# A decoder layer for two sequences: the loop over sequences written out as one straight program

## The chip, the cores and the metric

The kernel runs on one core of a Trainium2 chip. The metric is the device time of one execution in microseconds (us), median of three runs. A core has TensorE (PE, matrix products into eight accumulator banks of 128 x 512 fp32), VectorE (DVE), ScalarE (ACT), GpSimd (POOL) and SyncE (SP, which here only issues DMAs). Each engine has its own instruction stream, and they wait for each other through semaphores.

## What is computed

A post-layernorm decoder layer on x of 2 x 1024 x 256, all in fp32: causal self-attention with rotary embedding (16 heads of 16), cross-attention to 77 context tokens, and a gated feed-forward network of hidden width 1024 with ternary weights (times 8) and a scale for each output row. Each part is added to its input and normalised.

```python
x = _layernorm(x + attn(x, w_qkv, w_proj))          # softmax((q k^T)/4 under a causal mask) v
x = _layernorm(x + xattn(x, ctx, mask, Wq, bq, ..., Wo, bo))
# feed-forward, _tlin(x, w, s) = (x @ w.T) * s
h = silu(_tlin(x, w1_w, w1_s)) * _tlin(x, w2_w, w2_s)
h = gelu(_tlin(h, h1_w, h1_s))
h = gelu(_tlin(h, h2_w, h2_s))
x = _layernorm(x + _tlin(h, w3_w, w3_s))
```

## The kernel before, in words

`decoder_layer` sets up buffers and semaphores and runs a loop, `nc.Fori(0, BATCH)`, whose body `build_sequence` holds the whole work of one sequence for all five engines. Each turn begins after an all-engine barrier that also clears the semaphores. The body has these stages, on every engine in the same order:

- Projections. For each of 8 token tiles PE makes q and k (`project_qk`, L456, 512 wide) and, five tiles later, v (`project_v`, L463); the context's k and v (L470) come in between and are turned (`turn_ctx`). DVE applies the rotary embedding (`rope`, L980 to L982) and adds the context's biases and stages its k (`ctx_add`, L987 to L999); ACT copies v (`v_evac`, L849) and the turned context (`ctx_evac`, L857).
- Self-attention, in numbered steps. The heads go in 8 pairs. For a pair PE turns q and k (L507) and computes the raw scores once for the row maxima (L521, 24 units of up to 512 columns for each pair: "max units"). DVE reduces each unit (`reduce_unit`: L1028 where the whole bank is taken, L1030 with the causal mask and then a read of its accumulator). The first two pairs are done ahead of the first scores: the warm-up. `unit_bank` deals these 48 units over `SHARED` = 6 banks, and all later ones over banks 0 and 1, since banks 2 to 5 then hold scores. After the warm-up PE computes the scores again, transposed (L550), ACT takes their exp (L878), POOL clears above the diagonal (L1280), and PE multiplies by v (L567). Output projection, residual and layernorm of each token tile (`norm_products`, `norm_work`, `norm_evacs`) are put on fixed steps near the end of the attention.
- Cross-attention, built in the same way, with 3 max units for each pair, and its own projections and layernorms; the last four token tiles of those are interleaved with the first feed-forward products.
- Feed-forward in two chunks of 512 tokens. All operands are split into a high and a low part in a narrower type (fp32r), and each product is two matmuls of 512 columns (L733 for w1 and w2, L749 for h1 and h2, L761 for w3). A chunk has 36 groups, one bank each, taken in turn from six: 16 for w1 and w2 alternately (4 matmuls each), 8 for h1 and 8 for h2 (16 each), and 4 for w3 (16 each). ACT applies silu (L954) or gelu (L964), DVE multiplies silu by the second product (`gate`, L1224) and rounds to the high part (L1164), POOL subtracts for the low part (L1326). For w3, DVE multiplies by the scale (L1243), adds the residual (L1245), takes statistics (L1078, L1080), POOL makes the reciprocal root (`rstd`, L1286 to L1289), and DVE finishes (L1085), one tile later in its own order.

In the first turn alone, DVE looks through all feed-forward weights for bits that fp32r would lose (`check_piece`, L1074, 22 pieces) and every engine skips this by an `If(b == 0)` in the second turn. The weights (5.5 MB) are then resident in `ffn_w`. If bits were found, the feed-forward products run in fp32 on the same operands. The next sequence's tokens and context are loaded by SP while the last feed-forward products run.

## Time and profile before

| what | value |
|---|---|
| median of the runs | 972.98 us (972.43 to 979.55, 3 runs) |
| profiled execution | 979.19 us, of which its span (first to last instruction) 977.8 |
| TensorE busy | 882.5 us (90%), mean granted clock 0.895 |
| VectorE busy | 538.2 us (55%) |
| ScalarE busy | 364.8 us (37%) |
| GpSimd busy | 363.0 us (37%) |
| data moved | 34.61 MB |

The span can be cut into 40 equal slices. In the page's second section each digit is the busy share of a slice in tenths, and PEclk is the clock that TensorE was granted, in tenths of full speed:

```profile
PE   5879999888889999999968789999998889999997
DVE  3596788767676711441145967886167774116113
PEclk9965999769986999999979668997999699999999
DMA  9909201000000000000020000010000000000000
```

The first sequence takes slices 1 to 20 or so and the second the rest. The granted clock is given as a fraction of 2.4 GHz, so 0.5 is the lower of its two levels, 1.2 GHz, and a stretch with 0.74 is a mix.

### The profile page before, as it was taken

What the parts mean: (1) busy time and instruction counts of PE and PEld (TensorE: products, weight loads), DVE (VectorE), ACT (ScalarE), POOL (GpSimd) and SP (SyncE); (2) the same over time, 40 slices, a digit from 0 to 9 for tenths busy, and PEclk for the clock granted to TensorE, in tenths of its full rate; (3) what the DMA queues carried; (4) which work ended last, traced back from release to release, by engine and by line L of the source; (5) the groups of instructions that cost most, each with busy time, mean ns of one, the idle gap of its engine ahead of it and who ended that gap; (6) DMA issues with size and microseconds to landing.
All of it is one profiled execution on the core that took longest, in us unless ns stands there. A gap on an engine that the chain in (4) does not pass through costs nothing. (4 is left out here: it accounts for less than half of the span.)

```text
span 977.8 us, 13145 instructions
## 1 busy us (share of the span) xinstructions
PE 882.5 (90%) x4466; PEld 563.2 (58%) x4466; DVE 538.2 (55%) x1404; ACT 364.8 (37%) x770; POOL 363.0 (37%) x576
## 2 busy tenths in 40 slices
PE   5879999888889999999968789999998889999997
PEld 2545444334644788888745444543357257888886
DVE  3596788767676711441145967886167774116113
ACT  0314666454354421231103236665734443113110
POOL 4312224345345533353333122231362645335333
PEclk9965999769986999999979668997999699999999
DMA  9909201000000000000020000010000000000000
GB/s 305 336 7 401 72 2 46 2 1 1 2 5 0 1 1 1 1 1 1 22 94 1 1 2 2 2 45 2 1 1 4 3 1 1 1 0 22 1 1 24
DMA packets 15973, 34.61 MB, mean 35 GB/s; under 512 B 3483, under 2 KB 12392, under 8 KB 15720
## 3 DMA queue, kind: packets, MB, share of 16 engines
...
q8 instruction: 42, 0.69, 0.3%
...
## 5 line engine op out<-in xcount | busy, mean ns | idle before, releaser
L749 PE MATMUL bank<-hid_lo,ffn_w 128*128 128x512 f32 x512 | 202.2, 395 | 0.0
L878 ACT ACTIVATE prob<-bank 128x512 f32<-128x512 f32 (+3 forms) x384 | 164.2, 496 | 101.6 <-PE bank L550 100.9
L749 PE MATMUL bank<-hid_hi,ffn_w 128*128 128x512 f32 x512 | 201.6, 394 | 0.0
L1326 POOL TENSOR_TENSOR hid_lo<-act_raw,hid_hi 128x512 fp32r<-128x512 f32 x96 | 123.9, 1290 | 182.4 <-DVE hid_hi L1164 182.4
L1164 DVE CAST hid_hi<-act_raw 128x512 fp32r<-128x512 f32 x96 | 41.7, 435 | 212.4 <-ACT act_raw L964 211.3
L521 PE MATMUL bank<-k_t,q_t 64*128 64x512 f32 (+3 forms) x384 | 145.0, 496 | 13.0 <-DVE max_raw L1030 8.5
L1280 POOL TENSOR_SCALAR_AFFINE_SELECT prob<-prob 128x128 f32<-128x128 f32 x256 | 84.0, 344 | 180.5 <-ACT prob L878 177.9
L1030 DVE CUSTOM_DVE_ANT_0 bank<-bank,causal_bf 128x128 f32<-128x128 f32 (+3 forms) x256 | 122.3, 512 | 28.9 <-PE bank L521 26.8
L550 PE MATMUL bank<-q_t,k_t 64*128 64x512 f32 (+3 forms) x384 | 123.8, 438 | 0.9 <-issue 0.5
L964 ACT ACTIVATE act_raw<-bank,scales 128x512 f32<-128x512 f32 x64 | 44.2, 690 | 193.1 <-PE bank L749 193.1
L550 PEld LDWEIGHTS bank<-q_t,k_t 64*128 64x128 f32 x384 | 63.3, 211 | 82.5 <-ACT prob L878 47.5
L749 PEld LDWEIGHTS bank<-hid_lo,ffn_w 128*128 128x128 f32 x512 | 95.9, 187 | 23.9
L749 PEld LDWEIGHTS bank<-hid_hi,ffn_w 128*128 128x128 f32 x512 | 95.9, 187 | 23.3
L567 PE MATMUL bank<-prob,v_sb 128*32 128x512 f32 (+3 forms) x768 | 94.3, 567 | 8.6 <-POOL prob L1280 8.3
L1028 DVE TENSOR_REDUCE max_raw<-bank 128x1 f32<-128x512 f32 x128 | 82.4, 685 | 33.6 <-PE bank L521 33.6
L521 PEld LDWEIGHTS bank<-k_t,q_t 64*128 64x128 f32 x384 | 68.3, 222 | 52.0 <-DVE max_raw L1030 27.1
L456 PE MATMUL bank<-w_qkv,x_t 128*128 128x512 f32 x64 | 35.3, 698 | 22.0 <-issue 9.7
L733 PE MATMUL bank<-x_hi,ffn_w 128*128 128x512 f32 x128 | 51.3, 400 | 2.6 <-DVE x_lo L1147 2.6
L1318 POOL TENSOR_TENSOR prob<-prob,xmask_t 77x512 f32<-77x512 f32 x32 | 39.1, 1240 | 35.4 <-ACT prob L908 35.4
L733 PE MATMUL bank<-x_lo,ffn_w 128*128 128x512 f32 x128 | 50.6, 395 | 0.0
L908 ACT ACTIVATE prob<-bank 77x512 f32<-77x512 f32 x64 | 32.7, 591 | 25.9 <-PE bank L676 25.8
L1287 POOL TENSOR_SCALAR var_eps<-mean_var 128x1 f32<-128x1 f32 x48 | 15.1, 315 | 73.2 <-DVE mean_var L1080 73.1
...
## 6 DMA issues: line engine op xcount, KB each, us to landing
...
ffn_w<-scratch_w SPq DMA_DIRECT2D x3, 1024.0 KB, 7.0
x_t<-in_x_t SPq DMA_DIRECT2D x2, 1024.0 KB, 5.2
x_tok<-in_x SPq DMA_DIRECT2D x2, 1024.0 KB, 5.5
...
q_t<-max_rows SPq DMA_DIRECT2D x64, 4.0 KB
qx_t<-max_rows SPq DMA_DIRECT2D x64, 4.0 KB
...
```

Source lines behind the costliest of these rows:

```text
L521: mm(out[:, 0:k1 - k0], qkt(p, 0)[r, P * qt:P * (qt + 1)], qkt(p, 1)[r, k0:k1], start=True, stop=True).then_inc(S["max_mm"], 1)
L550: mm(S_BANK[j][:, 0:CHUNK - q0], qkt(p, 1)[r, P * kb:P * (kb + 1)], qkt(p, 0)[r, CHUNK * c + q0:CHUNK * (c + 1)], start=True, stop=True).t ...
L567: m = mm(Y_BANK[32 * j:32 * (j + 1), q0:CHUNK], v_window(v_sb[:, kb], 4 * g + j), prob[4 * (s % 2) + j][:, 0:CHUNK - q0], start=kb == 0, s ...
L733: o = mm(out[:], w_view(i, dt)[:, k, P * m:P * (m + 1)], view(x_hl[part][:, k, tokens]), start=k + part == 0, stop=(k, part) == (KD - 1, 1))
L749: o = mm(out[:], w_view(2 + layer, dt)[:, k, P * m:P * (m + 1)], view(src[part][:, k]), start=k + part == 0, stop=(k, part) == (KH - 1, 1))
L878: act.activation(prob[4 * (s % 2) + j][:, 0:n], S_BANK[j][:, 0:n], ACT.Exp, scale=SCALE).then_inc(S["exp_done"], 1)
L964: act.activation(act_raw[r % 3][:], bank[n % FFN_BANKS][:], ACT.Gelu, scale=scales[:, 2 + layer, m:m + 1]).then_inc(S["ffn_act"], 1)
L1028: dve.tensor_reduce(dst, unit_bank(n)[:], AXX, ALU.max).then_inc(S["max_red"], 1)
L1030: dve.tensor_tensor_reduce(out=unit_bank(n)[:, 0:left], in0=unit_bank(n)[:, 0:left], in1=L["causal_bf"][:, CHUNK - left:CHUNK], scale=1.0, ...
L1164: dve.tensor_copy(dst, act_raw[r % 3][:]).then_inc(S["act_hi"], 1)
L1280: pool.affine_select(out=pr, in_=pr, compare_op=ALU.is_ge, fill=0.0, base=0, pattern=[[1, P]], channel_multiplier=-1).then_inc(S["select_d ...
L1326: pt(dst[1][:, r % 8], act_raw[n % 3][:], dst[0][:, r % 8].bitcast(F32), ALU.subtract).then_inc(S["act_lo"], 1)
```

## The change

The loop becomes one straight program, `build_layer`, with the stages in the same order: all of sequence 0, then all of sequence 1. The barrier, the clearing of semaphores and the branches on `b` go. Every semaphore counts through both sequences (`wait(eng, q, name, n)` waits for `PER[name] * q + n`). Each sequence has an arena of 93,184 bytes of each partition for its buffers. The feed-forward weights are not resident: they are stored as 22 tiles of 512 KB. Sequence 0 reads them through a ring of four tiles that lie in the arena of sequence 1, and sequence 1 reads all of them from "home" tiles in the arena of sequence 0, which are loaded in the course of sequence 1's self-attention. Tokens and context of sequence 1 are loaded ahead of sequence 0's cross-attention. The branch on the found bits is taken once, ahead of the first feed-forward product, and the rest of the program lies behind it.

The order of work comes from `SLOTS` (a list of steps) and `PLAN` (which groups of feed-forward products lie in which slots). In each slot PE runs the other stage's part, the feed-forward products of `F_MM[slot]`, and then the norm products; ACT and DVE take up a group in the slot after the one in which it is done (`F_AFTER`), and DVE finishes a w3 tile one slot later still (`F_FINISH`), ahead of the slot's other groups.

```diff
-SHARED = 6
+QK_BANKS = ((2, 3), (0, 1))
+V_BANKS = ((4, 5), (6, 7))
+CTX_BANKS = ((0, 1), (6, 7))
+SHARED = (6, 2)
+XSHARED_BANKS = 6
+F_BANKS = ((2, 3, 4, 5), (0, 1, 2, 3, 4, 5))
...
+PLAN = [
+    (0, 0, ("w1", "w2"), ("N", 0, FFN_STEP), ("N", 0, X_END - 1)),
...
+    (1, 1, ("w3",), ("F", 1, 52), ("F", 1, 55)),
+]
...
+    for _j, (n, i) in enumerate(_work):
+        _k = max(_a + _j * (_b - _a + 1) // len(_work), F_DONE.get((_q, n - len(F_BANKS[_q])), -1) + 1)
+        F_MM[_k].append((_q, n, i))
+        F_START.setdefault((_q, n), _k)
+        F_DONE[_q, n] = _k
+F_AFTER = [[qn for qn in F_DONE if F_DONE[qn] == k - 1] for k in range(END_SLOT)]
+F_FINISH = [[qn for qn in F_DONE if F_DONE[qn] == k - 2 and GROUPS[qn[1]][1] == "w3"] for k in range(END_SLOT)]
...
+RING = 4
...
+RING_LAST = [max(n for n in range(len(GROUPS)) if r in ring_uses(n)) for r in range(NC * PIECES)]
...
-        with nc.Fori(0, BATCH) as b:
-            with nc.Block() as block:
-                build_sequence(nc, block, b, shared, S)
-            nc.all_engine_barrier(sems_to_clear=range(first, last + 1))
-        nc.sync.wait_ge(out_done, 16 * NT * BATCH)
...
+        def fill_ring(r):
+            if r >= RING:
+                wait(sp, 0, "f_mm", RING_LAST[r - RING] + 1)
+            if RING_MOVED[r]:
+                wait(sp, 1, "v_mm", NT)
+            sp.dma_start(ring_tile(r)[:], a["scratch"][r % PIECES]).then_inc(ring_in[r % RING], 16)
...
+        sp.wait_ge(S["check_op"], PIECES + 3)
+        load_tokens(1)
+        load_context(1)
+        for r in range(RING):
+            fill_ring(r)
...
+            if stage_name == "S":
+                attention(1, s)
+                if 4 <= s < 4 + PIECES:
+                    fill_home(s - 4)
...
     @block.scalar
...
+        def projections(q, t):
+            if t in (4, 5):
+                ctx_evac(q, t - 4)
+            if 0 <= t - V_LAG < NT:
+                v_evac(q, t - V_LAG)
...
     @block.vector
...
+        def f_work(slot):
+
+            for q, n in F_FINISH[slot]:
+                c, layer, m = GROUPS[n]
+                out_finish(q, 4 * c + m)
+            for q, n in F_AFTER[slot]:
...
+                if layer == "w3":
+                    wait(dve, q, "f_mm", n + 1)
+                    out_stats(q, 4 * c + m, f_bank(q, n)[:, 0:D])
```

Three excerpts of the engines' instruction order show where rows move. In their names a number behind the last underscore is only the program's own count, `_s0` and `_s1` are the sequence, and a bank is written with its number.

First excerpt, PE at the start of the self-attention's warm-up. Of the loop's body (both sequences ran it):

```order
L521 MATMUL bank0<-k_t0_55,q_t0_54 128x128
L521 MATMUL bank1<-k_t0_55,q_t0_54 128x128
L521 MATMUL bank2<-k_t0_55,q_t0_54 128x256
L521 MATMUL bank3<-k_t0_55,q_t0_54 128x256
L521 MATMUL bank4<-k_t0_55,q_t0_54 128x384
L521 MATMUL bank5<-k_t0_55,q_t0_54 128x384
L521 MATMUL bank0<-k_t0_55,q_t0_54 128x512
L521 MATMUL bank1<-k_t0_55,q_t0_54 128x512
L521 MATMUL bank2<-k_t0_55,q_t0_54 128x512
L521 MATMUL bank3<-k_t0_55,q_t0_54 128x512
```

and now for sequence 1:

```order
L654 MATMUL bank0<-k_t0_s1_74,q_t0_s1_73 128x128
L654 MATMUL bank1<-k_t0_s1_74,q_t0_s1_73 128x128
L654 MATMUL bank0<-k_t0_s1_74,q_t0_s1_73 128x256
L654 MATMUL bank1<-k_t0_s1_74,q_t0_s1_73 128x256
L654 MATMUL bank0<-k_t0_s1_74,q_t0_s1_73 128x384
L654 MATMUL bank1<-k_t0_s1_74,q_t0_s1_73 128x384
L654 MATMUL bank0<-k_t0_s1_74,q_t0_s1_73 128x512
L654 MATMUL bank1<-k_t0_s1_74,q_t0_s1_73 128x512
L654 MATMUL bank0<-k_t0_s1_74,q_t0_s1_73 128x512
L654 MATMUL bank1<-k_t0_s1_74,q_t0_s1_73 128x512
```

The units are the same; they are dealt over banks 0 and 1 where they went over banks 0 to 5. For sequence 0 they still go over six.

Second excerpt, DVE at the w3 tiles of the first chunk. `resid_f0` and `resid_f1` are the two buffers of a tile's residual. Before:

```order
L1243 TENSOR_TENSOR resid_f1_108<-bank3,scale_w3 128x256
L1245 TENSOR_TENSOR resid_f1_108<-resid_f1_108,tok 128x256
L1078 BN_STATS stats<-resid_f1_108 128x6
L1080 BN_AGGR mean_var<-stats 128x2
L1085 TENSOR_SCALAR tok<-resid_f0_107,mean_var,rstd 128x256
L1243 TENSOR_TENSOR resid_f0_107<-bank4,scale_w3 128x256
L1245 TENSOR_TENSOR resid_f0_107<-resid_f0_107,tok 128x256
L1078 BN_STATS stats<-resid_f0_107 128x6
L1080 BN_AGGR mean_var<-stats 128x2
L1085 TENSOR_SCALAR tok<-resid_f1_108,mean_var,rstd 128x256
L1243 TENSOR_TENSOR resid_f1_108<-bank5,scale_w3 128x256
L1245 TENSOR_TENSOR resid_f1_108<-resid_f1_108,tok 128x256
```

and now:

```order
L1360 BN_STATS o_stats<-resid_f0_s0_151 128x6
L1362 BN_AGGR o_mean<-o_stats 128x2
L1369 TENSOR_SCALAR tok0<-resid_f0_s0_151,o_mean,o_rstd 128x256
L1356 TENSOR_TENSOR resid_f1_s0_152<-bank3,scale_w3 128x256
L1358 TENSOR_TENSOR resid_f1_s0_152<-resid_f1_s0_152,tok0 128x256
L1360 BN_STATS o_stats<-resid_f1_s0_152 128x6
L1362 BN_AGGR o_mean<-o_stats 128x2
L1369 TENSOR_SCALAR tok0<-resid_f1_s0_152,o_mean,o_rstd 128x256
L1356 TENSOR_TENSOR resid_f0_s0_151<-bank4,scale_w3 128x256
L1358 TENSOR_TENSOR resid_f0_s0_151<-resid_f0_s0_151,tok0 128x256
L1360 BN_STATS o_stats<-resid_f0_s0_151 128x6
```

The finish of a tile (the TENSOR_SCALAR into `tok`) stood behind the next tile's statistics; it now stands directly behind its own tile's, ahead of the next tile's multiply.

Third excerpt, ACT where the first feed-forward products meet the last norm steps of the cross-attention. `x_hi` and `y_t` belong to the norm steps, `silu_sb` to the w1 groups. Before:

```order
L894 ACTIVATE x_hi_97<-bank0 128x2x128
L954 ACT_TABLE_LOAD
L954 ACTIVATE silu_sb_106<-bank0,scales 128x512
L887 ACTIVATE y_t1_82<-bank6 128x256
L894 ACTIVATE x_hi_97<-bank6 128x2x128
L954 ACTIVATE silu_sb_106<-bank2,scales 128x512
L894 ACTIVATE x_hi_97<-bank6 128x2x128
L954 ACTIVATE silu_sb_106<-bank4,scales 128x512
```

and now, for sequence 0:

```order
L1057 ACTIVATE x_hi_s0_147<-bank0 128x2x128
L1050 ACTIVATE y_t1_s0_120<-bank6 128x256
L1057 ACTIVATE x_hi_s0_147<-bank6 128x2x128
L1081 ACT_TABLE_LOAD
L1081 ACTIVATE silu_sb_s0_173<-bank2,scales 128x512
L1081 ACTIVATE silu_sb_s0_173<-bank4,scales 128x512
L1057 ACTIVATE x_hi_s0_147<-bank6 128x2x128
L1081 ACTIVATE silu_sb_s0_173<-bank2,scales 128x512
```

The silu of a group stood ahead of the norm evacuations of its own step; it now stands behind the whole of those, at the start of the next slot, and the groups of sequence 0 go over banks 2 to 5 in place of six. The table load that goes with silu moves with it.

## Rows read from the trace of the kernel before

**Rows 1.** Busy time by window: window, length, PE, PEld, DVE, ACT, POOL, clock, DMA share, GB/s.

```profile
80.00:100.00 20.00, 19.29 (x92) 9.97 (x96) 13.33 (x43) 10.84 (x25) 5.59 (x16) 0.59 1.02 408
342.40:494.60 152.20, 150.14 (x705) 122.87 (x703) 36.61 (x84) 31.44 (x43) 58.75 (x55) 1.00 0.04 13
536.80:550.00 13.20, 9.79 (x40) 5.54 (x38) 13.09 (x46) 2.39 (x4) 1.45 (x2) 0.74 0.00 0
575.00:595.00 20.00, 19.29 (x92) 9.88 (x96) 13.30 (x44) 10.76 (x25) 5.54 (x16) 0.59 0.01 3
595.00:615.00 20.00, 19.25 (x129) 8.61 (x121) 15.49 (x47) 12.59 (x30) 6.08 (x18) 0.99 0.01 2
802.00:820.20 18.20, 17.88 (x83) 14.25 (x83) 12.72 (x27) 7.76 (x15) 9.94 (x12) 1.00 0.00 0
```

**Rows 2.** Timeline around the loop's turn: start, us, operation, count, idle before and releaser.

```profile
488.99 0.42 DVE L1243 TENSOR_TENSOR resid_f<-bank,scale_w 128x256 f32<-128x256 f32 x1 [2.01 <-PE bank L761]
...
494.85 0.42 DVE L1243 TENSOR_TENSOR resid_f<-bank,scale_w 128x256 f32<-128x256 f32 x1
...
504.35 6.53 PE L456 MATMUL bank<-w_qkv,x_t 128*128 128x512 f32 x8 [9.74 <-issue]
...
517.78 0.68 DVE L980 TENSOR_TENSOR rope_a<-bank,cos_t 128x512 f32<-128x512 f32 x1
```

**Rows 3.** Timeline of DVE and ACT in the third pair of sequence 1, first exp.

```profile
566.10 0.14 DVE L1030 DVE_READ_ACCUMULATOR2_ANT max_raw<- 128x1 f32 x1
...
567.13 0.70 DVE L1030 CUSTOM_DVE_ANT_0 bank<-bank,causal_bf 128x512 f32<-128x512 f32 x1 [0.37 <-PE bank L521]
...
568.76 1.34 DVE L1028 TENSOR_REDUCE max_raw<-bank 128x1 f32<-128x512 f32 x2 [0.23 <-PE bank L521]
...
570.86 0.30 DVE L1030 CUSTOM_DVE_ANT_0 bank<-bank,causal_bf 128x128 f32<-128x128 f32 x1 [0.75 <-PE bank L521]
...
572.10 1.29 DVE L1028 TENSOR_REDUCE max_raw<-bank 128x1 f32<-128x512 f32 x2 [0.63 <-PE bank L521]
...
571.39 0.60 ACT L878 ACTIVATE prob<-bank 128x512 f32<-128x512 f32 x1 [0.34 <-PE bank L550]
```

**Rows 4.** Timeline of DVE at the last w3 tiles of the program.

```profile
966.77 0.42 DVE L1243 TENSOR_TENSOR resid_f<-bank,scale_w 128x256 f32<-128x256 f32 x1 [2.01 <-PE bank L761]
...
970.63 0.42 DVE L1243 TENSOR_TENSOR resid_f<-bank,scale_w 128x256 f32<-128x256 f32 x1
...
972.61 0.42 DVE L1243 TENSOR_TENSOR resid_f<-bank,scale_w 128x256 f32<-128x256 f32 x1
...
973.99 0.18 DVE L1080 BATCH_NORM_AGGREGATE mean_var<-stats 128x2 f32<-128x6 f32 x1
...
975.24 0.41 DVE L1085 TENSOR_SCALAR tok<-resid_f,mean_var,rstd 128x256 f32<-128x256 f32 x1 [0.75 <-POOL rstd L1289]
```

**Rows 5.** Timeline of ACT and PE at the end of sequence 0's projections.

```profile
37.85 0.38 ACT L849 ACTIVATE v_sb<-bank 128x256 f32<-128x256 f32 x1
...
38.29 1.09 PE L507 MATMUL bank<-ident,stage_q 128*128 128x128 f32 x8 [1.08 <-ACT v_sb L849]
```

**Rows 6.** ACT at the first silu of sequence 1 (timeline); costliest groups of the page.

```profile
801.00 1.28 ACT L954 ACT_TABLE_LOAD   x1
803.07 0.69 ACT L954 ACTIVATE silu_sb<-bank,scales 128x512 f32<-128x512 f32 x1 [0.79 <-PE bank L733]
...
L1326 POOL TENSOR_TENSOR hid_lo<-act_raw,hid_hi 128x512 fp32r<-128x512 f32 x96 | 123.9, 1290 | 182.4 <-DVE hid_hi L1164 182.4
L1164 DVE CAST hid_hi<-act_raw 128x512 fp32r<-128x512 f32 x96 | 41.7, 435 | 212.4 <-ACT act_raw L964 211.3
```

**Rows 7.** Chain that ended last (start, us), and DVE's timeline at chunk 1's first gate.

```profile
888.90 14.94 PE bank L733 x64
...
892.10 0.74 DVE L1224 SCALAR_TENSOR_TENSOR act_raw<-bank,scales,silu_sb 128x512 f32<-128x512 f32 x1
```

**Rows 8.** DMA issues of the page: count, KB each, us to landing.

```profile
x_t<-in_x_t SPq DMA_DIRECT2D x2, 1024.0 KB, 5.2
```

More of the change, by code:

```diff
@@ L168, in decoder_layer @@
+assert all(RING_SLOT[r] <= F_START[0, n] for n in range(len(GROUPS)) for r in ring_uses(n))
 def decoder_layer(nc, a):
@@ new lines, in build_layer, with wait, first_sequence_done, qkt @@
+    w_in, out_done, set_pool, set_dve = L["w_in"], L["out_done"], L["set_pool"], L["set_dve"]
+    A_BANK, Y, R = [bank[i] for i in A_BANKS], bank[Y_BANK], bank[R_BANK]
+    S_BANK = [bank[i] for i in S_BANKS]
+    def wait(eng, q, name, n):
+        eng.wait_ge(S[name], PER[name] * q + n)
+    def first_sequence_done(eng):
+        wait(eng, 0, "x_lo", NT)
+    def round_bank(n, early):
+        return Y if n < early and n % 2 else R
+    def qkt(q, p, which):
+        return turned[q][p % QKBUF][which]
@@ L447, in _ @@
+        for k in range(len(SLOTS), END_SLOT):
+            for i, n in F_FINISH[k - 1]:
+                c, layer, m = GROUPS[n]
+                store(i, 4 * c + m)
+        sp.wait_ge(out_done, 16 * NT * BATCH)
     @block.tensor
@@ new lines, in _ @@
+        pe.wait_ge(set_pool, 10)
+        pe.wait_ge(set_dve, 3)
+        wait(pe, 0, "x_t_in", 16)
+        pe.wait_ge(L["w_qkv_in"], 16)
+        for t in range(NT + V_LAG):
+            projections(0, t)
+        pe.wait_ge(w_in, 16 * 7)
+        for s in range(FIRST_STEP, S_END):
+            attention(0, s)
+        pe.wait_ge(S["check_op"], PIECES + 3)
+        wait(pe, 0, "q_add", NT)
+        mm(S_BANK[3][0:1, 0:1], low_max[:], L["ones"][:], start=True, stop=True).then_inc(S["flag_mm"], 1)
@@ new lines, in _ @@
+        last = L["causal_bf"][:, CHUNK - P:CHUNK]
+        pool.affine_select(out=last, in_=last, compare_op=ALU.is_ge, fill=NEG, base=0,
+                           pattern=[[-1, P]], channel_multiplier=1).then_inc(set_pool, 1)
+        fill(0)
+        pool.memset(low_bits[:], 0).then_inc(S["check_op"], 1)
+        for t in range(NT):
+            projections(0, t)
+        pool.wait_ge(w_in, 16 * 7)
+        for s in range(FIRST_STEP, S_END):
+            attention(0, s)
+        pool.wait_ge(S["check_op"], PIECES + 3)
```

1486 lines of the change are left out of this document (799 added, 687 removed), and 13 rows, old and new, of the table PLAN.

## Prediction

> **What bounds the kernel now.** I read first the windows by stage, then the timeline at the places where a stage changes hands. In both sequences TensorE (PE) is the bound nearly everywhere: the feed-forward stretch 342.40 to 494.60 has 150.14 us of matmul in 152.2 us, all at a granted clock of 1.00 [rows 1]. Three places are different, and the change touches all of them. (1) The turn of the loop: PE stands still for 9.74 us before 504.35, and then the first eight matmuls take 6.53 us, 0.82 each, which is the 1.2 GHz level [rows 2]. (2) The warm-up of each attention, where row maxima are taken before the first scores: VectorE (DVE) is busy 13.09 of 13.20 us for one pair of heads, so DVE sets the pace while PE works ahead of it by six banks; the clock falls there (0.74) [rows 1, 3]. (3) The layernorms beside the w3 products: DVE needs 1.98 us for a token tile, PE 1.87, and the last tile's chain ends the program [rows 4].
>
> **The change, part by part.** All positions are those of the profiled execution (979.19 us for its span of 977.8).
>
> *The seam, −11.3.* Stores, barrier, semaphore clear and loop branch go; the last w3 matmul (end 494.6) is followed at once by project_qk of sequence 1. What is late next is DVE, because the w3 tail is reordered: out_finish(i−1) now stands ahead of out_stats(i) (second excerpt of the order), so each tile waits for GpSimd's rstd. In the tail a last multiply at 972.61 is followed by its aggregate at 973.99 and its finish at 975.24, so multiply to finish is 2.63 and with the 0.4 of the finish a tile takes 3.0 in place of 1.98 [rows 4]. Multiply 0 is at 488.99 [rows 2]; multiply 3 moves from 494.85 to 488.99 + 3 × 3.0 = 498.0, its aggregate ends at 499.6, and only then rope(0) can run. From there: rope(0) to 500.95, out_finish(3) to 501.3, rope(1) to 502.6, rope(2) after PE's third pair (501.0 + 1.75 + 0.2) to 504.25, ctx_add 2.15, rope(3) at 506.4. Before, rope(3) started at 517.78 [rows 2]. PE is warm (no idle ahead of it), so its own work, 10.5 us, fits in. 517.78 − 506.4 = 11.4; I take 11.3.
>
> *Context evacuations earlier, −1.1.* ScalarE (ACT) does ctx_evac before the v evacuations, not between the last three. Before, the last v copy ran 37.85 to 38.23 and PE started at 38.29 [rows 5]; its products ended at 37.2, so the copy can end at 37.65. 0.55 per sequence.
>
> *Two banks in the warm-up of sequence 1, +10.4.* SHARED is (6, 2): the first 48 max units use bank 0 and 1 alone (first excerpt). The trace shows this regime in pair 2, from 563.4 on, without scores at first: DVE idles 0.37 before the 512-wide unit at 567.13, 0.23 at 568.76, 0.75 at 570.86 (a set of transposes between), and 0.63 at 572.10 [rows 3]. From the end of a unit to the start of the one two later it is 0.9 us for 512 columns (566.24 to 567.13) and about 0.5 to 0.6 for 128 or 256. A pair has twelve couples of units: the idle ahead of them, in order, is 0, 0.23, 0 (stage casts cover it), 0.37, 0.23, 0.75, 0.57, 0.6, 0.5, 0.66, 0.36, 0.9, together 5.2. Two pairs: 10.4, all on the path, since DVE sets it. Bounds: 0 if DVE never waits; 10.4 at the low clock, about 5 if PE stays at 2.4 GHz, as PE's part of each idle halves.
>
> *A table load ahead of the first exp of sequence 1, +0.9.* The old loop body began with a load where ACT was idle; now the load stands directly before exp. A load is 1.28 [rows 6], and ACT waited 0.34 there [rows 3]: 0.9 is left.
>
> *Feed-forward slots of chunk 0, +6.2 and +1.5.* Now 13 products run, then the norm products, and ACT and DVE take up a slot's groups only after that slot's norm work (third excerpt). Sequence 0 has four banks, sequence 1 six. Count from the first product: 0.233 per product (14.94 for 64 [rows 7]). Slot 0 ends on PE at 4.25 (3.03 + 1.2 of norms). ACT ends xt_evac at 4.75, loads the table to 6.03, silu(0) to 6.72. Group 4 wants the bank of group 0: PE waits from 4.95 to 6.8 (1.85). Gate(0) 6.77 to 7.5, norm products to 10.2. Then DVE does residual(7), which waits for PE's projection, finish and x_lo, until 12.0, and only then gate(1), to 12.75, which frees group 3's bank: PE waits from 10.67 to 12.8 (2.1). In slot 3 silu(3) frees bank 4 at 16.8 (1.0 of wait), in slot 4 gate(4) ends at 21.55 (1.65). The 64 products and norms end at 24.35; before it was 18.2 [rows 1]. With 0.25 at the first h1 group, whose last part waits for hid_lo (1.29 on GpSimd behind a 0.43 cast, itself behind gate(7) [rows 6]), less some small waits now gone, +6.2. With six banks only a wait of 0.3 is left, but PE is then ahead of the evacuations and the first h1 group waits 1.8 for hid_lo 6 and 7: +1.5. Lower bound of both together: 0, if ACT and DVE are not held back by the norms; upper bound: two slots' whole evacuation, some 12.
>
> *w3 to chunk 1, +2.5 and +0.6.* Gate(0) of chunk 1 was at 892.10 with PE starting chunk 1 at 888.90 [rows 7]. DVE's serial tail moves the gate to 895.25. With four banks group 39 waits for multiply 3 (892.7, due 891.7: 1.0) and group 41 for the gate's end at 896.0 (1.4); with six, group 43 waits 0.6.
>
> *The end, +3.1.* Multiply 0 of the last four tiles stays at 966.77; finish(3) starts at 966.77 + 9.0 + 2.63 = 978.4 in place of 975.24 [rows 4].
>
> *The ring, the home tiles, the loads: 0.* A ring tile is 512 KB and lasts 16 products, 3.7 us; it is refilled when the tile three others are ahead, so 11 us are there. A load of 1024 KB landed in 5.2 us [rows 8]. Traffic costs PE nothing either: 80 to 100 has DMA share 1.02 and the same 92 matmuls as 575 to 595 with 0.01 [rows 1]. If that cover were gone, each of 40 refills could cost a microsecond or two. The 22 home loads of 512 KB are issued between row moves that have three steps of slack; the second fill on GpSimd lies in idle time of its own. Added waits on ring_in are hidden: a group with sixteen waits runs at the same 0.233 as others.
>
> Sum: −11.3 − 1.1 + 10.4 + 0.9 + 6.2 + 1.5 + 2.5 + 0.6 + 3.1 = **+12.8**. The profiled execution would be 979.19 + 12.8 = 992.0; the median of the unprofiled runs is 972.98, 6.2 below it, and I carry the difference over: **985.8 us**. A measurement here tells about 1% (9.7 us) from no change.
>
> **Rivals.**
> (a) *The clock stays up in sequence 1's attention: 973.8, not slower.* Before, sequence 1 started cold after 9.7 us of stillness; now it starts warm. From 575 to 595 the clock is 0.59 and 92 matmuls fit in 20 us, from 595 to 615 it is 0.99 and 129 fit [rows 1]. If the low level did not come, the 24 us from the first score to 595 would shrink by 29%, 7.0, and the two-bank idle by 5: 985.8 − 12.0. Against it: the clock stood at 0.74 from 536.8 to 550 [rows 1], 30 us after the cold start, because DVE sets the pace in the warm-up; with two banks PE is busy for less. It decides if the clock over sequence 1's warm-up is above 0.9. Chance 0.12.
> (b) *The clock falls in the feed-forward stalls: 992.* In 802.00 to 820.20 PE was busy 17.88 of 18.20 at 1.00; in 536.8 to 550 it was busy 9.79 of 13.20, 0.74, at 0.74 [rows 1]. With my stalls sequence 0 has 17.9 of 24.4 busy, 0.73, like the second row. If a third to a half of these 24 us run at 1.2 GHz, 6 to 9 us of matmul grow by as much, part of it inside the stalls: +4 to +8. The Trainium skill (TensorE: Matmul & The Clock Gate, "A second HAM failure mode: psum-queue depth-cycling") says that short idles between matmul groups that cycle through banks make the clock swing between its two levels; by it this rival would be the forecast, at 992, while the row at 1.00 above gives 985.8. Chance 0.14.
> (c) *DVE and ACT hide most of the two-bank and slot waits: 977.5, no change.* If the idle of the warm-up is half of mine (5.2) and the slot stalls are 4.6 in place of 7.7, the sum is +4.5. For it: four of the twelve waits are measured [rows 3], the other eight are my reckoning. Chance 0.2.
> (d) *Nothing gained at the seam: 997.* The first projection finds another wait (a load, DVE's tail). The loads are issued 240 us earlier, so only chance 0.04 is left.
>
> **How the numbers follow.** Forecast 0.5: 981 to 990. The range must leave out 2 in 10: from 974 (case a) to 995 (case b's top). Slower by over 1% begins at 982.7: nearly nine tenths of the forecast (0.44), b and d, 0.62 together. Within 1%: a, c and the rest of the forecast, 0.34. Faster by over 1% needs a case a with every other loss small: 0.04.
>
> **What the new profile would show.** PE idle before sequence 1's first matmul under 1 us, and its first eight matmuls about half of 6.53 us; a tile of w3 on DVE every 3.0 us with an idle of 0.75 released by GpSimd; about 10 us of DVE idle, released by PE, in sequence 1's warm-up and none in sequence 0's; PE waiting about 6.6 us for ACT and DVE before the w1 and w2 products of sequence 0's chunk 0; a table load directly before the first exp of sequence 1. PE waits released by a ring load, or a clock that differs from the rows above in the warm-up or the slots, would make the sum wrong.

## The result: half of the forecast loss

The changed kernel takes 979.58 us (median of 18 runs, 977.75 to 983.28), the kernel before 974.11 (18 runs beside them, 967.23 to 980.24). The ratio is 1.0067 with a 95% interval of 1.0048 to 1.0086: slower by 6.5 us (by the medians, 5.5), forecast 12.8. It lies within the range of the prediction, and within the 1% that was called no change; the likeliest case, slower by more than 1%, did not come. The first profile of before was a long execution (979.19, five over the median); that of after, 979.01, is at its median. So the two spans are nearly equal, and they are compared below stretch by stretch.

The head of the page after:

```profile
span 977.2 us, 13096 instructions
PE 877.4 (90%) x4466; PEld 563.3 (58%) x4466; DVE 543.5 (56%) x1404; ACT 364.5 (37%) x770; POOL 360.3 (37%) x575
...
PE   5879999898889699999988889998988999999996
...
DVE  5597888677677421351165778786258664117113
...
PEclk9957999779977999999998569899999599999999
DMA  9909001003100134344300004640000000000000
```

TensorE has five microseconds of work less than before and the same share of the span. The windows of after, in the columns of [rows 1], cut where a stage begins on TensorE: warm-up, rest of the self-attention, slots, and remaining feed-forward part of sequence 0; projections, warm-up, rest of the self-attention of sequence 1; its slots, its feed-forward part, the tail. The windows of the warm-ups begin with the first max unit:

```profile
39.90:74.30 34.40, 27.32 (x98) 15.33 (x99) 32.08 (x110) 5.45 (x11) 4.49 (x6) 0.62 0.30 103
74.30:182.20 107.90, 103.17 (x619) 49.97 (x619) 84.40 (x257) 68.15 (x157) 29.58 (x91) 0.90 0.28 107
...
319.20:344.00 24.80, 18.73 (x83) 14.31 (x84) 11.90 (x26) 7.98 (x13) 9.24 (x11) 1.00 0.19 65
344.00:496.00 152.00, 147.52 (x706) 123.25 (x705) 36.57 (x82) 32.13 (x44) 59.35 (x55) 1.00 0.40 133
496.00:521.90 25.90, 23.89 (x83) 13.52 (x81) 17.71 (x44) 4.76 (x12) 11.81 (x12) 1.00 0.05 16
525.10:572.20 47.10, 37.46 (x98) 20.25 (x99) 34.31 (x110) 5.47 (x11) 4.59 (x6) 0.54 0.01 1
572.20:677.70 105.50, 100.28 (x619) 48.78 (x620) 84.38 (x257) 69.26 (x158) 29.58 (x91) 0.93 0.34 121
...
797.20:815.30 18.10, 18.10 (x83) 14.26 (x84) 10.32 (x24) 7.33 (x12) 7.80 (x10) 1.00 0.00 1
815.30:969.20 153.90, 148.09 (x705) 123.02 (x703) 38.14 (x84) 32.81 (x45) 60.77 (x56) 1.00 0.02 5
969.20:977.20 8.00, 0.00 (x0) 0.00 (x0) 3.66 (x11) 0.00 (x0) 1.56 (x4) 0.73 0.16 51
```

Each stretch, before and after, from the first instruction of one stage on TensorE to that of the next (us):

| stretch | before | after | difference | forecast |
|---|---|---|---|---|
| projections of sequence 0 | 28.8 | 27.3 | -1.5 | -0.55 |
| its warm-up to the first score | 37.4 | 37.7 | +0.3 | 0 |
| first score to last max unit | 111.1 | 107.9 | -3.2 | 0 |
| to its first w1 product | 137.3 | 136.9 | -0.4 | 0 |
| w1 and w2 of chunk 0 (slots) | 18.3 | 24.8 | +6.5 | +6.2 |
| to its last w3 product | 152.2 | 152.2 | 0.0 | +2.5 |
| last w3 product to first turn of sequence 1 | 38.6 | 25.7 | -12.9 | -11.85 |
| warm-up of sequence 1 | 37.4 | 50.3 | +12.9 | +10.4 |
| first score to last max unit | 111.1 | 105.5 | -5.6 | +0.9 |
| to its first w1 product | 120.1 | 119.4 | -0.7 | 0 |
| w1 and w2 of chunk 0 | 18.3 | 18.1 | -0.2 | +1.5 |
| to its last w3 product | 152.2 | 153.9 | +1.7 | +0.6 |
| tail | 5.4 | 8.0 | +2.6 | +3.1 |

The seam closed as the sum had it. TensorE goes from w3 to the projections without a pause, and its first eight products take 3.60 us where they took 6.53 [rows 2]; VectorE's `out_finish` waits for GpSimd ahead of every multiply (timeline of VectorE, then of TensorE):

```profile
490.42 0.42 DVE L1356 TENSOR_TENSOR resid_f_s<-bank,scale_w 128x256 f32<-128x256 f32 x1 [2.00 <-PE bank L889]
...
492.98 0.41 DVE L1369 TENSOR_SCALAR tok<-resid_f_s,o_mean,o_rstd 128x256 f32<-128x256 f32 x1 [1.00 <-POOL o_rstd L1518]
493.31 0.42 DVE L1356 TENSOR_TENSOR resid_f_s<-bank,scale_w 128x256 f32<-128x256 f32 x1
...
495.84 0.41 DVE L1369 TENSOR_SCALAR tok<-resid_f_s,o_mean,o_rstd 128x256 f32<-128x256 f32 x1 [0.98 <-POOL o_rstd L1518]
496.17 0.42 DVE L1356 TENSOR_TENSOR resid_f_s<-bank,scale_w 128x256 f32<-128x256 f32 x1
...
495.98 3.60 PE L587 MATMUL bank<-w_qkv,x_t_s 128*128 128x512 f32 x8
...
501.89 5.42 PE L587 MATMUL bank<-w_qkv,x_t_s 128*128 128x512 f32 x12 [0.59 <-DVE rope_b_s L1165]
```

The multiplies of the w3 tiles are 2.88 us apart (1.98 in [rows 4], 3.0 forecast). From a tile's multiply to its finish it is 2.56 where 2.63 had been reckoned: the wait for the root is 1.00 and not 0.75, but no finish of the tile before lies in between any more. The next multiply starts 0.33 behind the start of the finish. At the end of the program the same chain runs from 963.47, the first multiply, to 974.62, the last finish: 11.15 in place of 8.47 (timeline of VectorE).

```profile
963.47 0.42 DVE L1356 TENSOR_TENSOR resid_f_s<-bank,scale_w 128x256 f32<-128x256 f32 x1 [2.01 <-PE bank L889]
...
966.03 0.41 DVE L1369 TENSOR_SCALAR tok<-resid_f_s,o_mean,o_rstd 128x256 f32<-128x256 f32 x1 [0.99 <-POOL o_rstd L1518]
966.36 0.42 DVE L1356 TENSOR_TENSOR resid_f_s<-bank,scale_w 128x256 f32<-128x256 f32 x1
...
974.62 0.41 DVE L1369 TENSOR_SCALAR tok<-resid_f_s,o_mean,o_rstd 128x256 f32<-128x256 f32 x1 [0.97 <-POOL o_rstd L1518]
```

The warm-up of sequence 1 has a wait of VectorE ahead of nearly every couple of units. The values of [rows 3] (0.37, 0.23, 0.75, 0.63) come again in its second pair, from 548.80 on, as 0.37, 0.24, 0.76 and 0.64; the wider units behind them wait as follows in the first pair (timeline of VectorE, and of ScalarE at the first exp):

```profile
535.68 0.43 DVE L1215 CUSTOM_DVE_ANT_0 bank<-bank,causal_bf 128x256 f32<-128x256 f32 x1 [0.51 <-PE bank L654]
...
537.05 1.29 DVE L1213 TENSOR_REDUCE max_raw<-bank 128x1 f32<-128x512 f32 x2 [0.50 <-PE bank L654]
...
539.09 0.56 DVE L1215 CUSTOM_DVE_ANT_0 bank<-bank,causal_bf 128x384 f32<-128x384 f32 x1 [0.75 <-PE bank L654]
...
540.60 1.29 DVE L1213 TENSOR_REDUCE max_raw<-bank 128x1 f32<-128x512 f32 x2 [0.37 <-PE bank L654]
...
542.88 0.70 DVE L1215 CUSTOM_DVE_ANT_0 bank<-bank,causal_bf 128x512 f32<-128x512 f32 x1 [0.99 <-PE bank L654]
...
572.65 1.28 ACT L1041 ACT_TABLE_LOAD   x1
573.95 1.09 ACT L1041 ACTIVATE prob_s<-bank 128x512 f32<-128x512 f32 x2
```

Behind the first unit there are 22 such waits with 11.64 us together (before, 4 with 1.00): 5.0 in the first pair and 5.6 in the second, where 5.2 had been reckoned, and the rest at the start of the third. VectorE's busy time rose from 32.09 to 34.31 for the same 110 instructions. Their durations add to 42.1 us in both; as one that has waited no longer overlaps the one before it, less of that is hidden. The table load stands directly ahead of the first exp, 572.65, as forecast, and from the first score to the first exp it is 1.75 us where it was 0.79: 0.96 for the forecast 0.9.

In the slots of sequence 0 TensorE waits four times for the late evacuations, at the groups that were named (timeline of TensorE):

```profile
326.20 0.50 PE L880 MATMUL bank<-x_hi_s,ring_s 128*128 128x512 f32 x1 [1.77 <-ACT silu_sb_s L1081]
...
332.13 0.50 PE L880 MATMUL bank<-x_hi_s,ring_s 128*128 128x512 f32 x1 [1.81 <-DVE act_raw_s L1385]
...
336.29 0.50 PE L880 MATMUL bank<-x_hi_s,ring_s 128*128 128x512 f32 x1 [0.89 <-ACT silu_sb_s L1081]
...
341.12 0.50 PE L880 MATMUL bank<-x_hi_s,ring_s 128*128 128x512 f32 x1 [1.59 <-DVE act_raw_s L1385]
```

That is 6.06 us of idle together, where 6.6 was forecast. The clock of the stretch is 1.00, as the window of 319.20 shows.

### The profile page after: what moved, and what is told of

It is laid out like the page before. It is cut to its first block, busy times and chain, and to the rows that moved or that the text cites. A ratio compares the mean times of both kernels' runs of the same rounds, so it can differ in the third digit from the quotient of the medians.

```text
span 977.2 us, 13096 instructions
## 1 busy us (share of the span) xinstructions
PE 877.4 (90%) x4466; PEld 563.3 (58%) x4466; DVE 543.5 (56%) x1404; ACT 364.5 (37%) x770; POOL 360.3 (37%) x575
## 4 chain that ended last, share of the span: by engine, by line
PE 70%; DVE 18%; POOL 5%; issue 4%; ACT 3%; DMA 1%; SPq 0%; DVEq 0%; POOLq 0%; ACTq 0%
PE bank L892 22%; PE bank L654 7%; PE bank L685 6%; PE bank L702 6%; DVE bank L1215 5%; PE bank L880 4%; PE bank L640 3%; DVE max_raw L1213 3%; PE bank L587 3%; PE bank L889 3%; PE bank L825 3%; PE bank L775 2%; PE bank L735 2%; PE bank L833 2%; POOL prob_s L1501 1%
## 5 line engine op out<-in xcount | busy, mean ns | idle before, releaser
L1041 ACT ACTIVATE prob_s<-bank 128x512 f32<-128x512 f32 (+3 forms) x384 | 163.8, 497 | 92.0 <-PE bank L685 91.5
L1530 POOL TENSOR_TENSOR hid_lo_s<-act_raw_s,hid_hi_s 128x512 fp32r<-128x512 f32 x96 | 123.9, 1291 | 171.7 <-DVE hid_hi_s L1392 148.7
L654 PE MATMUL bank<-k_t_s,q_t_s 64*128 64x512 f32 (+3 forms) x384 | 151.8, 500 | 20.9 <-DVE max_raw L1215 15.9
L1501 POOL TENSOR_SCALAR_AFFINE_SELECT prob_s<-prob_s 128x128 f32<-128x128 f32 x256 | 83.2, 341 | 170.6 <-ACT prob_s L1041 168.1
L1392 DVE CAST hid_hi_s<-act_raw_s 128x512 fp32r<-128x512 f32 x64 | 27.3, 427 | 203.9 <-ACT act_raw_s L1087 203.9
L1215 DVE CUSTOM_DVE_ANT_0 bank<-bank,causal_bf 128x128 f32<-128x128 f32 (+3 forms) x256 | 122.3, 510 | 31.4 <-PE bank L654 29.9
L685 PE MATMUL bank<-q_t_s,k_t_s 64*128 64x512 f32 (+3 forms) x384 | 118.9, 423 | 0.9 <-issue 0.5
L892 PE MATMUL bank<-hid_hi_s,home_s 128*128 128x512 f32 x256 | 100.0, 391 | 3.6 <-POOL hid_lo_s L1530 3.5
L892 PE MATMUL bank<-hid_hi_s,ring_s 128*128 128x512 f32 x256 | 99.8, 390 | 0.7 <-POOL hid_lo_s L1530 0.7
L892 PE MATMUL bank<-hid_lo_s,home_s 128*128 128x512 f32 x256 | 99.6, 389 | 0.0
L892 PE MATMUL bank<-hid_lo_s,ring_s 128*128 128x512 f32 x256 | 99.6, 389 | 0.0
L702 PE MATMUL bank<-prob_s,v_sb_s 128*32 128x512 f32 (+3 forms) x768 | 89.8, 542 | 8.0 <-POOL prob_s L1501 7.7
L892 PEld LDWEIGHTS bank<-hid_hi_s,ring_s 128*128 128x128 f32 x256 | 48.0, 188 | 11.5 <-issue 1.5
L1071 ACT ACTIVATE prob_s<-bank 77x512 f32<-77x512 f32 x64 | 32.7, 590 | 25.7 <-PE bank L813 25.6
```

What stands on the lines that cost most here:

```text
L654: mm(out[:, 0:k1 - k0], qkt(q, p, 0)[r, P * qt:P * (qt + 1)], qkt(q, p, 1)[r, k0:k1], start=True, stop=True).then_inc(S["max_mm"], 1)
L685: mm(S_BANK[j][:, 0:CHUNK - q0], qkt(q, p, 1)[r, P * kb:P * (kb + 1)], qkt(q, p, 0)[r, CHUNK * c + q0:CHUNK * (c + 1)], start=True, stop=T ...
L702: m = mm(Y[32 * j:32 * (j + 1), q0:CHUNK], v_window(v_sb[q][:, kb], 4 * g + j), prob[q][4 * (s % 2) + j][:, 0:CHUNK - q0], start=kb == 0, ...
L892: o = mm(out[:], view(tile_h(f_weights(q, n, 0)[:], k), True), view(src[part][:, k]), start=i == 0, stop=i == last)
L1041: act.activation(prob[q][4 * (s % 2) + j][:, 0:n], S_BANK[j][:, 0:n], ACT.Exp, scale=SCALE).then_inc(S["exp_done"], 1)
L1215: dve.tensor_tensor_reduce(out=out[:, 0:left], in0=out[:, 0:left], in1=L["causal_bf"][:, CHUNK - left:CHUNK], scale=1.0, scalar=NEG, op0=A ...
```

## The experiments

All measure the whole computation. Times are medians; the runs of before beside them had medians of 973.9 to 975.4. "Stretch" is one of the table's.

### Two banks for the max units

The changed kernel, six banks again (`six_units`):

```diff
-SHARED = (6, 2)
+SHARED = (6, 6)
```

> The changed kernel with the max units of sequence 1's warm-up dealt over six banks again (as in sequence 0). Theory A, all of the warm-up's loss is time lost: from the first turn product to the first score takes 37.4 us in place of 50.3, and the rest stays: the program ends 12.9 us sooner, near 967. Theory B, part of the loss comes back because TensorE's clock rises sooner behind a slow warm-up (first score to last max unit took 105.5 us in place of 111.1 before): the warm-up gives 12.9 and that stretch takes 5.6 of it back, 7.3 us sooner, near 972. Theory C, two banks cost nothing and the low clock alone (0.54 in place of 0.66) made the warm-up long: its DVE idle stays and the time stays at 979.

Measured: 964.44 us (961.94 to 972.80, 10 runs), 0.991 of before (0.987 to 0.994). The warm-up takes 37.7 us. The 15.1 us to after are the whole loss and 2 more, so nothing "comes back" later: theory A. In this profile the stretch behind the warm-up took 108.0 in place of 105.5, which theory B wanted, and the one behind it 122.7 in place of 119.4; but that profile (972.8) is the longest of the ten runs, so the verdict goes by the medians.

The loop with two banks (`two_units_loop`), where the number serves self-attention and cross-attention:

```diff
-SHARED = 6
+SHARED = 2
```

> The kernel before with all max units of the warm-ups, self-attention and cross-attention, over two banks, nothing else changed. Theory A, each self-attention warm-up takes 12.9 us longer and nothing comes back: +26, near 999. Theory B, the clock rises sooner behind each: +7 for each sequence, +15, near 988. In both the cross-attention's warm-up (3 units for a pair) adds 0 to 3 for each sequence.

Measured: 1002.94 us (4 runs), ratio 1.032 (1.023 to 1.040), 29 us slower. Both warm-ups take 50.7 us, as its windows show (from first turn to first score):

```profile
36.90:87.50 50.60, 39.87 (x114) 22.09 (x115) 34.35 (x110) 7.60 (x15) 4.51 (x6) 0.56 0.27 91
...
544.00:594.70 50.70, 40.39 (x115) 22.43 (x115) 34.38 (x110) 7.69 (x15) 4.50 (x6) 0.54 0.00 1
```

VectorE is busy 34.35 and 34.38, as in the changed kernel; the cost of 13 us for a warm-up hangs on nothing else of the change. The cross-attention's part is in the stretches that hold it, 3.4 us longer in sequence 1 (120.1 to 123.5) and 1.9 in sequence 0; TensorE's waits for VectorE's maxima that were not there before add to 2.2 us in each. The 1.9 and 3.4 as they stand can't be put down to the banks, as these stretches also move by 2 to 3 us in kernels in which they are unchanged (122.7 in `six_units`).

Four banks (`four_units`, `SHARED = (6, 4)`):

> The changed kernel with sequence 1's max units over four banks, between two (first turn to first score 50.3 us, the time 979.6) and six (37.7, 964.4). Theory A, what two banks lack is that the matmul of the next couple of units can run while VectorE reduces this one, and four banks give that: 38 us and 965. Theory B, a longer lead is needed to cover the transposes and the bank hand-over: between 41 and 46 us, and 968 to 974.

Measured: 966.68 us (10 runs). The warm-up takes 40.7 us, 3 more than with six: closer to theory A, and not quite it. Eight waits of VectorE are left behind the first unit, 3.6 us together, the longest of them (0.78, 0.72, 0.48, 0.45) ahead of 256-wide couples. Of the 12.6 us that six banks save in the warm-up, two more banks give 9.6 and the last two 3.0.

### The slots

Six feed-forward banks for sequence 0 (`six_ffn`):

```diff
-F_BANKS = ((2, 3, 4, 5), (0, 1, 2, 3, 4, 5))
+F_BANKS = ((0, 1, 2, 3, 4, 5), (0, 1, 2, 3, 4, 5))
```

> The changed kernel with six banks in place of four for the feed-forward groups of sequence 0, the slots as they are. Theory A, the four banks make the late evacuations visible: the stretch from the first w1 product to the first h1 product falls from 24.8 to 18.1 as in sequence 1, the program ends 6.5 us sooner, near 973. Theory B, the place of silu and gate behind the norm work is enough by itself: the stretch stays above 22 us and the time within 3 us of 979.6.

Measured: 972.54 us (10 runs). The slots take 18.1 us, theory A; but the stretch behind them grew from 152.2 to 155.5, because TensorE is now ahead of the evacuations and waits at the first h1 group for GpSimd's low parts (its timeline):

```profile
340.86 0.47 PE L892 MATMUL bank<-hid_hi_s,ring_s 128*128 128x512 f32 x1 [0.93 <-POOL hid_lo_s L1530]
...
342.49 0.47 PE L892 MATMUL bank<-hid_hi_s,ring_s 128*128 128x512 f32 x1 [0.92 <-POOL hid_lo_s L1530]
```

At the first h1 group of chunk 1 it then waits 0.67 and 0.92, while the waits at the turn to chunk 1 (0.64 and 1.07) shrink to one of 0.19. Together that is 3.3 us, half of the 6.7. The same waits stand in sequence 1 of the changed kernel in both chunks. The stretches thus give 3.4 us and the medians 7.0. This profile (975.61) is 3.1 over its median, and what lies between the two figures is not traced to a stretch.

ScalarE, VectorE and GpSimd take up a group in its own slot where norm work is interleaved (`silu_first`), with four banks:

```diff
-F_AFTER = [[qn for qn in F_DONE if F_DONE[qn] == k - 1] for k in range(END_SLOT)]
+IN_SLOT = {k for k, slot in enumerate(SLOTS) if slot[0] == "N"}
+F_AFTER = [[qn for qn in F_DONE if (k if k in IN_SLOT else k - 1) == F_DONE[qn] and (k in IN_SLOT or F_DONE[qn] not in IN_SLOT)] for k in range(END_SLOT)]
```

> The changed kernel with ScalarE, VectorE and GpSimd taking up the groups of a slot ahead of that same slot's norm work (as the loop did), for the slots in which feed-forward products and norm steps meet; sequence 0 keeps its four banks. Theory A, the late place of silu and gate makes the four banks too few: with silu at its group's end the stretch from first w1 to first h1 product falls from 24.8 to about 19, the time by 5 to 6 us, to 974. Theory B, four banks are too few by themselves under slots of 13 products: the stretch stays at 22 or more and the time within 3 us of 979.6.

Measured: 971.94 us (10 runs). The slots take 17.6 us with four banks, less than before's 18.3 with six (its window):

```profile
321.00:338.60 17.60, 17.60 (x83) 14.35 (x84) 12.37 (x27) 6.91 (x14) 9.70 (x11) 1.00 0.27 90
```

So four banks are enough if the place of silu and gate is right, and with the late place six banks take the stall out of the slots too but have half of it come back. The loss needs both the late place and the four banks. Here nothing is handed back: 151.6 us behind the slots, and in sequence 1 17.6 and 151.4 in place of 18.1 and 153.9.

### VectorE's order at w3

Statistics of a tile ahead of the finish of the one before (`stats_first`):

```diff
         def f_work(slot):
 
-            for q, n in F_FINISH[slot]:
-                c, layer, m = GROUPS[n]
-                out_finish(q, 4 * c + m)
             for q, n in F_AFTER[slot]:
...
+            for q, n in F_FINISH[slot]:
+                c, layer, m = GROUPS[n]
+                out_finish(q, 4 * c + m)
```

> The changed kernel with VectorE's w3 work in the old order (statistics of tile i ahead of the finish of tile i-1). Theory A, the serial chain multiply to finish costs at each of four places: the end falls from 8.0 to 5.4 us behind the last product, the projections of sequence 1 from 25.9 to 24 (TensorE has 23.9 us of work there), and sequence 1's turn from chunk 0 to chunk 1 loses its 1.7: about 6 us sooner, near 973.5. Theory B, only the end is on the path: 2.6 us sooner, near 977.

Measured: 971.08 us (10 runs), 8.5 us below after. The tail falls from 8.0 to 5.9, the projections of sequence 1 from 25.9 to 25.0, the feed-forward parts from 152.2 to 149.5 and from 153.9 to 151.7: 7.9 together, so theory A, with the most of it (2.7 and 2.2) at and behind the turns from chunk 0 to chunk 1: in sequence 0 the waits of 0.64 and 1.07 are gone, in sequence 1 that of 0.19 and those at chunk 1's first h1 group (0.67 and 0.92). Theory A had 1.7 for this in sequence 1 and nothing in sequence 0, theory B nothing.

### All four undone

`all_undone` has the four edits together.

> The changed kernel with four parts as in the loop: six banks for sequence 1's max units, six for sequence 0's feed-forward groups, VectorE's statistics of tile i ahead of the finish of tile i-1, and silu and gate ahead of the same slot's norm work. Theory A, the losses are separate and add: from 979.6 it loses 15.1, 7.0 and 8.5 (the three measured one by one, the latter two by their medians) and comes to about 949 to 953. Theory B, they overlap (what the slots give is waited for again at the first h1 group, 3.3 us, and the low clock moves): 956 to 960.

Measured: 948.15 us (4 runs, 946.90 to 949.29), ratio 0.976 (0.970 to 0.983): faster than either kernel, by 26 us than before. (That it is more than 2% faster the interval leaves open.) One by one the edits had given 15.1, 8.5 and, for the slots, 7.0 or 7.6: 31 together, and 31.4 were found. They are separate and add, as theory A had it (theory B's 956 to 960 is 8 us off). The stretches that the edits touch, in its profile against after's, give 30.9. Its windows of the slots, the projections and the warm-up of sequence 1, and the tail:

```profile
317.80:335.40 17.60, 17.60 (x82) 14.39 (x83) 12.36 (x27) 6.94 (x14) 9.73 (x11) 1.00 0.27 90
484.20:509.20 25.00, 23.61 (x82) 13.60 (x80) 16.33 (x40) 4.76 (x12) 11.97 (x12) 1.00 0.05 16
509.20:547.30 38.10, 30.36 (x115) 17.70 (x115) 32.18 (x110) 7.66 (x15) 4.57 (x6) 0.57 0.01 2
939.20:945.00 5.80, 0.00 (x0) 0.00 (x0) 2.23 (x7) 0.00 (x0) 1.55 (x4) 0.68 0.23 72
```

So the straight program without these losses is worth 26 us: the seam some 13, 7 of the kind told next, and the rest, some 6, spread over the projections and the attentions. No run takes that rest apart.

### Six nanoseconds for each product

Nothing in the prediction had touched the duration of a matmul. Yet the feed-forward stretch of sequence 0 came out equal (152.2) with 2.4 us more of waits in it than before (4.42 for 2.06). Between two products of h1 and h2 pass 0.233 us before and 0.227 after, in both sequences, with loads running or not; the page's mean for one falls from 395 to 390 ns. The window from 346 to 396 of before, nothing but such products:

```profile
346.00:396.00 50.00, 50.00 (x216) 40.08 (x215) 5.94 (x14) 9.66 (x14) 16.70 (x13) 1.00 0.00 1
```

The same of after, where that phase lies 2 us later (350 to 400), and then its groups of h1 and h2 products by tile, with busy time, mean duration in ns, idle before and releaser:

```profile
350.00:400.00 50.00, 50.00 (x222) 41.40 (x221) 5.54 (x13) 9.44 (x14) 18.03 (x14) 1.00 0.44 146
```

```profile
L892 PE MATMUL bank<-hid_hi_s,home_s 128*128 128x512 f32 x256 | 100.0, 391 | 3.6 <-POOL hid_lo_s L1530 3.5
L892 PE MATMUL bank<-hid_hi_s,ring_s 128*128 128x512 f32 x256 | 99.8, 390 | 0.7 <-POOL hid_lo_s L1530 0.7
```

216 products in 50 us before, 222 after. For 1280 such products this is 7 us (1024 of h1 and h2 by 6.5 ns, 256 of w1 and w2 by 4.5, less half a microsecond for w3, which got slower by 2 ns each). Four kernels looked for the cause. The layout of the weights (`tiled_weights_loop`), in the loop:

```diff
+    def w_tile(i, m, dtype):
+        v = ffn_w[:, FO[i]:FO[i + 1]]
+        return (v if dtype is F32 else v.bitcast(dtype)).rearrange("p (m k n) -> p m k n", m=KH, n=P)[:, m]
...
-                                o = mm(out[:], w_view(2 + layer, dt)[:, k, P * m:P * (m + 1)], view(src[part][:, k]),
+                                o = mm(out[:], w_tile(2 + layer, m, dt)[:, k], view(src[part][:, k]),
```

(w1 and w2 and the loads likewise)

> The kernel before with w1, w2, h1 and h2 laid out in SBUF as the changed kernel has them (for each block of 128 outputs, the rows k one behind the other, 512 B apart, where they were 4 KB apart), nothing else changed. In the trace of before a feed-forward product starts every 0.233 us, in that of the changed kernel every 0.227. Theory A, the layout of the weights is the cause: 0.227 here too, 1280 products, about 7 us less, median near 967. Theory B, it is something else of the straight program (where tiles lie, how instructions are written): 0.233 and 974.

Measured: 975.12 us (10 runs), ratio 1.000 (0.996 to 1.005), 0.233 between products: theory B. Then the arena by 32 bytes, in the loop and, the other way, in the changed kernel:

```diff
-        arena = (nc.sbuf_base + 31) // 32 * 32
+        arena = (nc.sbuf_base + 31) // 32 * 32 + 32
```

> The kernel before with the start of its arena (the buffers of a sequence, the split activations of the feed-forward part among them) 32 bytes higher in SBUF: 135,264 in place of 135,232. In the changed kernel the arenas start at 40,160 and 133,344, both odd multiples of 32, in the kernel before at an even one. Laying out the weights otherwise left the products 0.233 us apart. Theory A, it is the place of the activations: products now start every 0.227 us, about 7 us less, 967. Theory B, it is something else of the straight program: 0.233 and 974.

Measured: 974.76 us (10 runs), ratio 0.999 (0.995 to 1.003). The products now start alternately 0.232 and 0.235 apart, with the same mean, so the offset is not the cause. The alternation itself can't be put down to it either: at the old addresses one chunk of sequence 1 has 0.231 and 0.236 in turn, the second in the first profile of before and the first in its second profile, and the other chunks have 0.233 throughout.

```diff
-        arena = [late + 8192, late + 8192 + ARENA]
+        arena = [late + 8224, late + 8224 + ARENA]
```

> The changed kernel with both arenas, and with them ring and home tiles, 32 bytes higher, at even multiples of 32 (40,192 and 133,376). Theory A, the place decides: products 0.233 us apart in place of 0.227, some 7 us more, near 987, and the stretches from first score to last max unit longer too (111 in place of 105 to 108) if their matmuls hang on it. Theory B: 0.227 and 979.6.

Measured: 978.93 us (10 runs), 0.227 as in after: theory B again. Last, weights and arena changed over (`weights_above_loop`), in the loop:

```diff
-        ffn_w = sb("ffn_w", [P, FO[5]], F32)
...
         arena = (nc.sbuf_base + 31) // 32 * 32
+        ffn_w = nc.alloc_sbuf_tensor_at("ffn_w", [P, FO[5]], F32, offset=arena + 93184)
```

> The kernel before with the feed-forward weights and the arena of the sequence's buffers changed over in SBUF: the arena starts at 45,120 (before: 135,232), the weights lie above it, at 138,304. Neither the layout of the weights nor 32 bytes of offset brought the products from 0.233 us apart to the 0.227 of the changed kernel. Theory A, it is where weights and activations lie (the weights of the kernel before lie at the low end, which no tile of the changed kernel uses for them): 0.227 here and 967. Theory B, it is the form of the program (loop against straight code): 0.233 and 974.

Measured: 966.16 us (5 runs), ratio 0.990 (0.986 to 0.993), and 222 products where there were 216 (its window):

```profile
346.00:396.00 50.00, 50.00 (x222) 41.44 (x221) 5.97 (x14) 9.39 (x14) 18.08 (x14) 1.00 0.00 0
```

Theory A: it is where tensors lie in SBUF. Each feed-forward stretch fell from 152.2 to 148.8, and 18.3 to 18.1, 7.2 us together (the medians are 9.2 apart). The edit moved three things at once: weights up, arena down, and the small tensors between them down by the 90,112 bytes of the weights. What about the place matters was not told apart. Neither simple reading is enough, the low address of the weights or the high one of the activations. In sequence 1 of the changed kernel the activations' arena starts at 133,344, only 1,888 bytes below that of before, and the home tiles of h1 lie from 56,544 to 89,312, across the h2 weights of before (50,304 to 83,072). Yet products are 0.227 apart there and 0.233 in before, for all of its h1 and h2 weights alike.

### The kernel before once more

> The kernel before once more, for a second profile. Theory A, the first profile (979.2 us) was a long execution by its clock alone: here the stretch from the first score to the last max unit is 105 to 108 in place of 111.1, with fewer low stretches of the clock, and everything else is as it was. Theory B, 111.1 is what the kernel before always takes there: it is 111 again in both sequences, and the changed kernel's 105.5 and 107.9 are a gain of the change.

Measured: 977.29 us, one run. The stretch from first score to last max unit is 109.7 and 111.0, near theory B; but over all kernels here it lies between 104.5 and 111.1, in sequence 0 where their instructions there are the same: 104.5 to 107.9 in the straight ones, and 105.1, 107.9, 109.5, 109.6, 109.7 and 111.1 in the loops. Part of that comes back in the stretch behind it: from first score to first w1 product it is 237.0 to 245.0 in the straight ones and 244.4 to 249.5 in the loops. What differs is TensorE's granted clock over it, 0.86 in both sequences of before, 0.90 and 0.93 after. The runs tell the same: of the 25 runs of before beside `six_units`, those with a mean clock of 0.910 to 0.912 took 966.2 to 967.6 us and those with 0.893 to 0.895 took 976.3 to 979.1. Why the straight program has the low level less often in that stretch stays open. By the medians it is worth about 3 us of the result: the table's other stretches add to +8.3, and 5.5 were measured.

## The prediction, step by step

**The seam** was right: -11.3 and -1.1 for the two context evacuations against -12.9 (and -1.5 in sequence 0's projections, of which the gap ahead of the first turn explains 0.56: 1.08 in [rows 5], 0.52 after; the rest can't be told from scatter, as the loops have 27.5 to 28.9 there and the straight kernels 26.6 to 28.0). Stores, barrier and cold clock were what it cost, and VectorE's tail was what came late next.

**Two banks** were right in mechanism, place and value: 10.4 for the idle, 10.64 measured, to which the lost overlap of VectorE's instructions adds 2.2. That was the part not reckoned. The table load behind it was right too (0.96 for 0.9), though the stretch that holds it came out shorter. The loop with two banks shows the price by itself.

**The slots** were right in sequence 0 (+6.5 for +6.2) and each wait was where the count had put it; the prediction named the four banks and the order together, and the runs show that both are needed. In sequence 1 the loss was not in the slots but behind them: 1.86 at the first h1 group of chunk 0 (forecast 1.8). In chunk 1 it was 0.19 at the gate (forecast 0.6) and 1.59 at the first h1 group, which was not forecast.

**w3 to chunk 1, the tail**: 0.64 and 1.07 of wait for the forecast 1.0 and 1.4, and 2.6 for 3.1. Undoing the order alone gives back 2.7 us at the turn to chunk 1 in sequence 0.

```profile
415.41 0.50 PE L880 MATMUL bank<-x_hi_s,ring_s 128*128 128x512 f32 x1 [0.64 <-DVE resid_f_s L1356]
...
418.60 0.50 PE L880 MATMUL bank<-x_hi_s,ring_s 128*128 128x512 f32 x1 [1.07 <-DVE act_raw_s L1385]
```

**Ring, home tiles, loads at nothing** was right as to waits: no product waits for a ring tile, which land in 3.3 us (11 were there), and products run at 0.227 with a DMA share of 0.40 as with 0.02. But of the sum, the term "the ring, the home tiles, the loads: 0" is the one that failed. It weighed waits and traffic, and not that the tiles and activations got other places in SBUF. By what `weights_above_loop` gains in the same stretches, that term is -7.2. It is as large as the difference between the 12.8 of the sum and the 5.5 that were measured (7.3) because the other misses happen to cancel. The warm-ups are 2.8 worse, the feed-forward waits 4.4 (15.2 with the 7.2 taken out, for 10.8: their idle is 11.5, and each product that has waited takes 0.47 to 0.50 in place of 0.39 and doesn't overlap the one before); projections and seam are 2.0 better, the tail 0.5. The two attentions, forecast at 0 apart from the table load, are 10.8 better in the two profiles. As the first profile of before was some 6 us longer against its median than that of after, 4.8 of this is left by the medians. That remainder is the second thing the sum lacked, and its cause (the granted clock there) is open. So the time lay within the stated range in part by luck.

**The rivals.** (a) The clock stays up: no. The warm-up of sequence 1, from its first max unit to the first score, ran at 0.54, nearly all of it at 1.2 GHz, although TensorE came to it warm (1.00 in the projections). Cut in the same way, warm warm-ups with six banks ran at 0.62 (`six_units`) and 0.53 (`all_undone`), and the loops behind their cold start at 0.66 in before and at 0.62, 0.64, 0.55 and 0.55 in four others. So a warm start does not keep the clock up, and the spread from 0.53 to 0.66 goes with neither the start nor the banks. (b) The clock falls in the stalls: no. TensorE was busy 18.73 of 24.80 us in the slots, a share of 0.76 with four waits of 0.9 to 1.8, and the clock stayed at 1.00; the swing between the two levels that the Trainium skill tells of (TensorE: Matmul & The Clock Gate, "A second HAM failure mode: psum-queue depth-cycling") did not show in this stretch. (c) named nearly the time that came (977.5 for 979.6) by a wrong reason: nothing was hidden, the waits came in full. That was luck. (d) did not come.
